# Second 16-head attention in a new order, its exponential at the eviction of the transposed scores, and the linear attention's end interleaved with the first cross attention

## The chip, the core and the metric

The kernel runs on one core of a Trainium2 chip. A core has five engines with a queue of instructions each: TensorE (PE: matrix products and transpositions, which go into eight PSUM banks), VectorE (DVE), ScalarE (ACT), GpSimd (POOL) and SyncE (SP), whose queue only starts transfers here. Every queue is written out by hand, and semaphores are all that orders one engine against another. The metric is device microseconds of one execution, lower being better.

## The reference

Two layers of a post-norm decoder over 16 sequences of 128 tokens and 256 features, in float32. Each of the six sublayers is added to its input and normalized:

```python
x = ln(x + linear_attention(x))      # A: 16 heads, rms norm of q and k, rotation, relu, no softmax
x = ln(x + cross_attention(x, ctx))  # B: one head, causal softmax
x = ln(x + sparse_ffn(x))            # C: 15 of 128 tokens of a sequence, 16-head attention and FFN
x = ln(x + self_attention(x))        # D: 16 heads of 16 features, softmax
x = ln(x + cross_attention(x, ctx))  # E: 16 heads of 16 features, causal softmax
x = ln(x + moe(x))                   # F: 16 experts, 4 of them per token, and two shared ones
```

D and E compute, for each sequence and each head, `softmax(q k^T * 16**-0.5) v`, and E also masks the keys behind the query. The first "16-head attention" of this text is D and the second is E. F's router is a product of the normalized result of E with a 256x16 matrix.

## The kernel before

A sequence (128 rows) is the unit of work and is called a turn, numbered 0 to 15. A stage is a function of a turn, with a lag: `pipelined` and `chained` run over iterations i and call each stage of their list for turn i minus its lag, in the list's order. Every engine has a list of its own, and what an iteration's list says is the order of that engine's queue. D and E are one `chained` loop of 32 turns on each engine, so that iterations 16 and above hold E's turn i - 16 for lag 0. Two places of the code matter most.

**The end of A and the begin of B.** A runs on PE as the list a_nd (lag 4), a_kv (3), a_qkp (0), a_atp (4), a_vp (1), a_op (4) in iterations 0 to 19. Behind it come four small products (`b_fold`) that multiply B's weight matrices with each other, two into bank 1 and two into bank 2, and then B's loop, which begins by transposing the normalized rows of turn 0 (b_turn). On ACT, A's last stage is a_final (lag 8, L1679), which writes the normalized row into X and needs the reciprocal root that POOL has worked out (a_power, L892 to L897, and DVE's y, L2041, waits for the a_final of two turns before, since there are two buffers). Behind all sixteen a_final stand the two copies of the folded weights (L1686, L1688) and then B's loop, with the copy of the transposed row (L1641) first. DVE's queue ends A with y, sum and statistics of turn 15, copies a column (L2096) and goes on to B's row maximum (L2059). The small first transfer of constants (cos and sin) and the second (identity, masks and others) are waited for as l_rows and l_const; DVE waits for both before its first work on a turn (L1994), POOL for l_const at its begin.

**A turn of D or E.** For four groups r of four heads each, PE computes the negated scores into banks 3 to 6 (L1493, and in E the mask, L1504). DVE takes the row minimum of each (L2416, L2418). For groups 0 to 2 ACT evicts the bank with `exp(min - s)`, four instructions of one head each (L1871); for group 3 DVE subtracts into SBUF (L2421) and ACT takes the exponential there (L1875). PE transposes the four heads of a group into bank 7 (d_pT, L1520), ACT copies the bank to SBUF (d_pTc, L1882), and since all groups share bank 7, group r + 1 is transposed only when group r is copied. Then PE multiplies with v (d_pv, L1530), DVE divides (d_div, L2427 to L2436), PE applies the output matrix (d_out), and DVE adds and takes statistics (d_y, L2443). The row transposition of a later turn (d_turn, L1036) and its projections (d_proj) stand in the same list; both write bank 1. In E the router of F follows three steps later in the same bank: f_turn transposes the normalized row (L1057), ACT copies it (f_copy, L1820), f_lg multiplies, and ACT copies the logits (f_logit, L1824). For turns 5 to 15 of E, d_turn waits until the logits of five turns before are copied, which are those of the same iteration (f_logit raises f_lc):

```python
def d_turn_(t, n=n, round=round):
    wait(pe, d_qkc.again(n), t, 4, back=1)
    if n == 1:
        wait(pe, f_lc, t, 1, back=5)
    turn_x(round, o=bank[1])(t)
```

From E's turn 9 on, DVE also does the first half of the routing between d_div and the next minimum (f_first_half).

## Time and profile before

| what | us |
|---|---|
| median of 3 runs | 896.17 |
| lowest and highest of them | 892.79, 896.87 |
| the profiled execution | 893.42 |
| its span, first to last instruction | 891.6 |

In that span PE is busy for 812.5 us (91%), DVE for 543.2, ACT for 509.6 and POOL for 457.4. The span falls into the linear attention A (to about 110), B (to about 185), C (to about 285), D (to about 405), E with the router (to about 560), the scattering of rows to the experts' lists (to about 645) and the experts with the final sum (to the end). Times below are microseconds from the begin of the span. A row of the timeline gives start, duration, engine, line, operation, output and inputs by the names of the program, shape and count; the bracket at its end is how long the engine stood idle before it and what released it. Most buffers are views of one tensor called arena.

### The profile page before, as it was taken

Reading aid. Unit: us, or ns where it says so; the run is one execution under the profiler, and the core shown is the slowest. Engines: PE = TensorE matmul, PEld = TensorE weight load, DVE = VectorE, ACT = ScalarE, POOL = GpSimd, SP = SyncE. Lnnn points to the kernel's source line nnn. Section 1 sums busy time; section 2 is a strip of 40 time slices with the busy share of each in tenths; the row PEclk is TensorE's granted clock in tenths of the full one; section 3 lists DMA queues with packets and bytes.
Section 4 is the critical chain, followed back from the end, with each engine's and each line's share of the span. In section 5 each row is a group of like instructions: output and inputs, shape, how many; then the busy total and the mean of one; then the engine's idle time right before and its main releaser. Section 6 shows DMA issues by size and latency. Waiting matters only on the chain.

```text
span 891.6 us, 21329 instructions
## 1 busy us (share of the span) xinstructions
PE 812.5 (91%) x6466; PEld 663.1 (74%) x6467; DVE 543.2 (61%) x1608; ACT 509.6 (57%) x1348; POOL 457.4 (51%) x609
## 2 busy tenths in 40 slices
PE   5989679998898999998999987999889999999995
PEld 2666569875687788877677765555889999999963
DVE  3788727857413788888877899586233333333325
ACT  2556445544524888888888866310555565556524
POOL 4988511201306465544456542777766555555545
PEclk9999989999799999999999999999999999999998
DMA  9620011000007999994611001637576555655556
GB/s 308 203 69 12 13 42 43 25 25 13 13 21 244 316 279 336 298 295 139 249 38 35 8 33 37 243 136 251 168 109 104 94 93 96 97 92 93 97 75 250
DMA packets 86645, 113.52 MB, mean 127 GB/s; under 512 B 8224, under 2 KB 77600, under 8 KB 86048
## 3 DMA queue, kind: packets, MB, share of 16 engines
q1 hardware_dynamic: 71392, 90.49, 33.7%
q0 software_dynamic: 14448, 19.34, 13.4%
q10 hardware_dynamic: 720, 2.63, 0.8%
q8 instruction: 44, 0.72, 0.4%
q14 instruction: 41, 0.34, 0.1%
HBM read 48.40 MB, written 64.05 MB: 126 GB/s over the span
## 4 chain that ended last, share of the span: by engine, by line
PE 57%; DVE 12%; POOL 11%; ACT 8%; issue 8%; DMA 4%; SPq 0%; DVEq 0%; ACTq 0%; POOLq 0%
PE bank L1044 39%; POOL grid L948 7%; PE bank L1520 4%; ACT arena L1871 4%; PE bank L1057 3%; PE bank L1493 3%; PE bank L1530 1%; DMA const<-in_const 1%; PE bank L1388 1%; ACT arena L1882 1%; POOL arena L894 1%; DMA arena<-ys 1%; DMA ys<-arena 1%; DVE arena L2416 1%; DVE arena L2006 1%
## 5 line engine op out<-in xcount | busy, mean ns | idle before, releaser
L1044 PE MATMUL bank<-arena 128*128 128x256 f32 (+6 forms) x1028 | 276.6, 403 | 13.8 <-ACT arena L1669 8.7
L1044 PEld LDWEIGHTS bank<-arena 128*128 128x128 f32 (+1 forms) x1028 | 175.5, 190 | 71.4 <-issue 38.1
L1004 POOL DMA_INDIRECT ys<-arena x79 | 123.1, 1558 | 95.1 <-DVE arena L2535 74.5
L1044 PEld LDWEIGHTS bank<-arena,rows 128*128 128x128 f32 x1264 | 153.5, 192 | 8.6 <-ACT arena L1910 3.2
L1044 PE MATMUL bank<-arena,rows 128*128 128x128 f32 x1264 | 155.8, 276 | 2.5 <-ACT arena L1910 2.5
L1871 ACT ACTIVATE arena<-bank,arena 128x128 f32<-128x128 f32 x384 | 114.0, 420 | 5.7 <-DVE arena L2416 5.6
L1920 ACT COPY rows<-arena 128x1024 f32 x79 | 82.6, 1045 | 33.3 <-issue 24.4
L2524 DVE TENSOR_TENSOR arena<-arena,bank 128x256 f32<-128x256 f32 x79 | 33.3, 422 | 106.1 <-ACT arena L1905 105.6
L853 POOL TENSOR_TENSOR lr<-mv,const 128x1 f32<-128x1 f32 x48 | 9.1, 191 | 171.8 <-DVE mv L1957 171.8
L1882 ACT COPY arena<-bank 128x512 f32<-128x512 f32 x128 | 79.8, 624 | 21.1 <-PE bank L1520 20.2
L1520 PE MATMUL bank<-const,arena 128*128 128x128 f32 x512 | 80.5, 280 | 12.4 <-ACT arena L1882 9.6
L1520 PEld LDWEIGHTS bank<-const,arena 128*128 128x128 f32 x512 | 56.1, 141 | 30.7 <-issue 20.4
L948 POOL DMA_INDIRECT grid<-X,arena x64 | 63.4, 991 | 20.2 <-issue 18.8
L1905 ACT ACTIVATE arena<-bank 128x256 f32<-128x256 f32 x79 | 30.4, 385 | 72.0 <-PE bank L1044 72.0
L2416 DVE TENSOR_REDUCE arena<-bank 128x4 f32<-128x512 f32 x96 | 62.2, 683 | 14.8 <-PE bank L1493 7.9
L1044 PE MATMUL bank<-arena,inT 128*128 128x256 f32 (+1 forms) x192 | 59.8, 436 | 9.3 <-DMA arena<-in_a_w 5.8
L1044 PE MATMUL bank<-xT,arena 128*128 128x128 f32 x512 | 66.5, 279 | 1.6 <-ACT xT L1641 1.6
L1044 PEld LDWEIGHTS bank<-xT,arena 128*128 128x128 f32 x512 | 62.3, 195 | 2.3 <-ACT xT L1641 2.3
L2535 DVE TENSOR_SCALAR arena<-bank,arena 128x256 f32<-128x256 f32 x79 | 38.2, 484 | 27.9 <-PE bank L1044 22.9
L1044 PEld LDWEIGHTS bank<-arena,inT 128*128 128x128 f32 x192 | 34.3, 198 | 18.9 <-issue 11.4
L1057 PE MATMUL bank<-const,arena 128*128 128x128 f32 x222 | 43.1, 276 | 4.4 <-DMA arena<-grid 2.3
L1836 ACT ACTIVATE arena<-bank 128x512 f32<-128x512 f32 x16 | 9.6, 598 | 63.8 <-PE bank L1044 63.8
(291 smaller groups left out, 1455.2 us busy)
## 6 DMA issues: line engine op xcount, KB each, us to landing
grid<-arena SPq DMA_DIRECT2D x1, 37264.0 KB, 133.9
arena<-in_f_w SPq DMA_DIRECT2D x18, 768.0 KB, 6.8
arena<-grid SPq DMA_DIRECT2D x79, 137.0 KB, 2.6
arena<-ys SPq DMA_DIRECT2D x8, 512.0 KB, 7.8
inT<-in_ctxT SPq DMA_DIRECT2D x30, 128.0 KB, 2.0
X<-in_x SPq DMA_DIRECT2D x1, 2048.0 KB, 15.7
arena<-in_c_w SPq DMA_DIRECT2D x2, 1024.0 KB, 5.4
ys<-arena SPq DMA_DIRECT2D x1, 2048.0 KB, 10.3
```

The costliest lines, as they stand in the source:

```text
L948: pool.indirect_dma_start(grid, bass.IndirectOffsetOnAxis(ap=f_to[:, b, k:k + 1], axis=0), X[:, b, :], None).then_inc(l_sc[b % 3], 16)
L1004: pool.indirect_dma_start(ys, bass.IndirectOffsetOnAxis(ap=number, axis=0), s_y[t.ring(YR)], None, compute_op=ALU.add).then_inc(l_sy[t.rin ...
L1044: m = pe.matmul(o, lhs[k], rhs[k], start=k == 0, stop=k == n - 1)
L1057: m = pe.transpose(o[:, k * width:(k + 1) * width], src(k), ident[0:width, 0:width])
L1520: m = pe.transpose(bank[7][:, i * P:(i + 1) * P], d_S[t.p][:, QH * r + i, :], ident)
L1871: m = act.activation(d_S[t.p][:, at, :], bank[3 + r][:, i * P:(i + 1) * P], ACT.Exp, bias=d_mx[t.p][:, at:at + 1], scale=-1.0)
L1882: act.copy(d_pT[t.p][:, QH * r:QH * (r + 1), :], bank[7][:].rearrange("p (a b) -> p a b", a=QH)).then_inc(d_pTc.sem, 1)
L1905: act.activation(f_h[t.p], bank[2 + t.p][:, 0:EF], ACT.Silu).then_inc(q_silu.sem, 1)
L1920: act.copy(f_up[t.p], W[:, bass.ds(e, 1), 0:2 * KC * EF].rearrange("p a n -> p (a n)")).then_inc(q_wc.sem, 1)
L2416: dve.tensor_reduce(mx, s_, AX.X, ALU.min).then_inc(dm.sem, 2)
L2524: dve.tensor_tensor(f_aT[t.p], f_h[t.p].rearrange("p (k t) -> p k t", k=KC), bank[2 + t.p][:, EF:2 * EF].rearrange("p (k t) -> p k t", k=K ...
L2535: dve.tensor_scalar(s_y[t.ring(YR)], bank[6 + t.p][:, 0:D], s_w[t.p], None, ALU.mult).then_inc(q_yc.sem, 1)
```

## The change

Four edits.

1. **Begin.** POOL's and DVE's waits for the second transfer of constants stand where the first of them is read: POOL's at the first a_power, DVE's at the first a_kvm.
2. **End of A.** The four folding products are taken into A's list on PE, one at the end of each of the iterations 16 to 19. ACT leaves A's loop with three a_final undone, copies the folded weights, enters B's loop and does the three at the ends of B's iterations 1, 2 and 3. DVE's first write of B's normalized row waits until all of A's are read.
3. **Exponential.** In D and E, ACT evicts the score banks 3 to 5 with `min - s` (Identity), DVE subtracts group 3 in that sense too, PE transposes these differences, and ACT takes the exponential when it evicts bank 7 (d_pTc). The separate exponential of group 3 (L1875) is gone, and the transposition of group 3 waits for DVE alone. The four evictions of group 2 are split: two as before at the end of an iteration, two in the next iteration behind the first d_pTc, where L1875 stood.
4. **Order of E.** On PE, d_out stands between the transpositions of groups 2 and 3, and f_lg behind that of group 3. On ACT, f_logit stands behind the eviction of group 1. D keeps its order.

The core of the diff:

```diff
-            chained(pe, [[(a_nd_, 4), (a_kv_, 3), (a_qkp_, 0), (a_atp_, 4), (a_vp_, 1), (a_op_, 4)]])
...
+            def b_fold_(i):
+                part = i - B
...
+                o, wl, wr = ((bank[1], b_wq, b_wk), (bank[2], b_wv, b_wp))[part // KC]
+                k = part % KC
+                m = product(o[:, k * D:(k + 1) * D], [wl[:, e, k * P:(k + 1) * P] for e in range(KC)],
+                            [wr[:, e, :] for e in range(KC)])
...
+            chained(pe, [[(a_nd_, 4), (a_kv_, 3), (a_qkp_, 0), (a_atp_, 4), (a_vp_, 1), (a_op_, 4)]], b_fold_)
...
-                        wait(pe, d_exp.again(n), t, r + 1)
+                        if direct(r):
+                            wait(pe, d_exp.again(n), t, r + 1)
+                        else:
+                            wait(pe, d_max.again(n), t, 2 * r + 2)
...
-                               (last(f_lg_), 7), (d_pT_(3), 5), (d_out_, 6), (d_turn_, 2), (d_pv_, 5), (last(f_first_pos_), 5),
+                               (last(d_out_), 6), (d_pT_(3), 5), (d_out_ if n == 0 else None, 6), (last(f_lg_), 7),
+                               (d_turn_, 2), (d_pv_, 5), (last(f_first_pos_), 5),
...
-            pipelined(act, [(a_final_, 8), (a_osq_, 5), (a_fTc_, 3), (a_sq_, 1), (a_relu_, 2), (a_atc_, 4)])
+            pipelined(act, [(a_final_, 8), (a_osq_, 5), (a_fTc_, 3), (a_sq_, 1), (a_relu_, 2), (a_atc_, 4)], left=A_LEFT)
...
+            def a_rest_(i):
+                if 0 < i <= A_LEFT:
+                    a_final_(turn(B - 1 - A_LEFT + i))
...
-                        act.copy(d_pT[t.p][:, QH * r:QH * (r + 1), :],
-                                 bank[7][:].rearrange("p (a b) -> p a b", a=QH)).then_inc(d_pTc.sem, 1)
+                        act.activation(d_pT[t.p][:, QH * r:QH * (r + 1), :], bank[7][:].rearrange("p (a b) -> p a b", a=QH),
+                                       ACT.Exp).then_inc(d_pTc.sem, 1)
...
-                rounds.append([(last(h_fill_(0)), 6), (d_pTc_(0), 5), (d_exp_(3), 5), (d_qkc_, 3),
+                early, late = range(QH // 2), range(QH // 2, QH)
+                rounds.append([(last(h_fill_(0)), 6), (d_pTc_(0), 5), (d_exp_(2, heads=late), 5), (d_qkc_, 3),
...
-                               (last(f_logit_), 7), (d_pTc_(3), 5), (d_exp_(1), 4),
-                               (copy_xT(round, before, reader, bank[1]), 2), (d_exp_(2), 4),
+                               (d_pTc_(3), 5), (d_exp_(1), 4), (last(f_logit_), 7),
+                               (copy_xT(round, before, reader, bank[1]), 2), (d_exp_(2, heads=early), 4),
```

ACT's queue in a turn of E, before. L1882 is d_pTc, L1871 the eviction of the scores of a group (one head and then three), L1820 f_copy, L1824 f_logit, L1641 the copy of the row that d_turn has transposed:

```order
L1820 COPY arena<-bank 128x256 [waits f_tp]
L1882 COPY arena<-bank 128x512 [waits d_pv,d_pTp]
L1871 ACTIVATE arena<-bank,arena 128x128 [waits d_pTp,d_max]
L1871 ACTIVATE arena<-bank,arena 128x128 x3
L1824 COPY arena<-bank 128x16 [waits f_lp]
L1882 COPY arena<-bank 128x512 [waits d_pv,d_pTp]
L1871 ACTIVATE arena<-bank,arena 128x128 [waits d_pTp,d_max]
L1871 ACTIVATE arena<-bank,arena 128x128 x3
L1641 COPY xT<-bank 128x256 [waits d_qkp,turned]
```

The same stretch of ACT's queue now, where the lines are L1837 (f_copy), L1896 (d_pTc), L1886 (evictions), L1841 (f_logit) and L1652:

```order
L1837 COPY arena<-bank 128x256 [waits f_tp]
L1896 ACTIVATE arena<-bank 128x512 [waits d_pv,d_pTp]
L1886 ACTIVATE arena<-bank,arena 128x128 [waits d_pTp,d_max]
L1886 ACTIVATE arena<-bank,arena 128x128 x3
L1896 ACTIVATE arena<-bank 128x512 [waits d_pv,d_pTp]
L1886 ACTIVATE arena<-bank,arena 128x128 [waits d_pTp,d_max]
L1886 ACTIVATE arena<-bank,arena 128x128 x3
L1841 COPY arena<-bank 128x16 [waits f_lp]
L1652 COPY xT<-bank 128x256 [waits d_qkp,turned]
```

The copy of the logits has moved from the place behind the first four evictions to the place behind the next d_pTc and four more evictions.

PE's queue in the same turn now, from the transposition of group 2 on (L1530 is d_pT, L1044 with 128x256 d_out, with 128x16 f_lg, L1036 d_turn, L1540 d_pv):

```order
L1530 MATMUL bank<-const,arena 128x128 [waits d_pTc,d_exp]
L1530 MATMUL bank<-const,arena 128x128 x3
L1044 MATMUL bank<-arena 128x256 [waits d_y,d_atc]
L1044 MATMUL bank<-arena 128x256
L1530 MATMUL bank<-const,arena 128x128 [waits d_pTc,d_max]
L1530 MATMUL bank<-const,arena 128x128 x3
L1044 MATMUL bank<-arena 128x16 [waits f_xt]
L1044 MATMUL bank<-arena 128x16
L1036 MATMUL bank<-const,xs 128x128 [waits copied,xt_done,f_lc,d_qkc]
L1036 MATMUL bank<-const,xs 128x128
L1540 MATMUL bank<-arena 32x128 [waits d_pTc,e_vc,d_bk]
```

Before, f_lg stood behind the first of these transpositions and d_out behind the second; d_turn with its wait for f_lc, and d_pv behind it, stand last in both.

PE's queue at the end of A now (L1092 is a_nd, L1057 from arena a_atp, L1044 waiting for a_ob a_op, the other L1044 folding products, L1057 from X the first of B):

```order
L1044 MATMUL bank<-arena 128x256 [waits a_ob,a_atc]
L1044 MATMUL bank<-arena 128x256
L1044 MATMUL bank<-arena 128x256 [waits a_vb]
L1044 MATMUL bank<-arena 128x256
L1092 MATMUL bank<-arena 128x136 [waits a_div,a_fTc,a_kvm]
L1092 MATMUL bank<-arena 128x136
L1057 MATMUL bank<-const,arena 128x128 [waits a_atc,a_div]
L1057 MATMUL bank<-const,arena 128x128
L1044 MATMUL bank<-arena 128x256 [waits a_ob,a_atc]
L1044 MATMUL bank<-arena 128x256 x3
L1057 MATMUL bank<-const,X 128x128 [waits normed]
```

Before, no folding product stood ahead of a_nd, and all of them stood behind the last a_op.

ACT's queue at the same place before (L1674 is a_osq, L1693 and L1699 are B's copy of the queries and its exponential):

```order
L1674 ACTIVATE arena<-arena 128x256 [waits a_pow,a_ob]
L1679 ACTIVATE X<-y,arena 128x256 [waits a_pow] x3
L1686 ACTIVATE arena<-bank 128x512 [waits b_fold]
L1688 COPY arena<-bank 128x512 [waits b_fold]
L1641 COPY xT<-bank 128x256 [waits turned] x2
L1693 COPY arena<-bank 128x256 [waits b_qp]
L1641 COPY xT<-bank 128x256 [waits b_qp,turned]
L1699 ACTIVATE arena<-arena 128x128 [waits b_max]
```

And now, with a_osq on L1687, a_final on L1692, the copies of the weights on L1699 and L1701, of the rows on L1652, of the queries on L1706:

```order
L1687 ACTIVATE arena<-arena 128x256 [waits a_pow,a_ob]
L1699 ACTIVATE arena<-bank 128x512 [waits b_fold]
L1701 COPY arena<-bank 128x512 [waits b_fold]
L1652 COPY xT<-bank 128x256 [waits turned] x2
L1706 COPY arena<-bank 128x256 [waits b_qp]
L1692 ACTIVATE X<-y,arena 128x256 [waits a_pow]
L1652 COPY xT<-bank 128x256 [waits b_qp,turned]
L1712 ACTIVATE arena<-arena 128x128 [waits b_max]
```

The three a_final have moved from the place ahead of the copies of the folded weights into B's loop, of which the first is seen here.

## Rows read from the trace of the kernel before

**Rows 1.** Timeline of the first 14 us: start, duration, engine, line, operation, count [idle].

```profile
12.23 0.69 DVE L1994 TENSOR_TENSOR arena<-bank,rows 128x512 f32<-128x512 f32 x1 [2.12 <-DMA const<-in_const]
```

**Rows 2.** Timeline from the end of A to the first turns of B.

```profile
103.24 0.63 PE L1092 MATMUL bank<-arena 128*128 128x136 f32 x4
...
103.91 0.17 DVE L2021 TENSOR_SCALAR arena<-bank 128x16 f32<-128x16 f32 x1
...
105.78 4.58 PE L1044 MATMUL bank<-arena 128*128 128x256 f32 x20 [0.46 <-ACT arena L1669]
...
107.41 0.42 ACT L1674 ACTIVATE arena<-arena 128x256 f32<-128x256 f32 x1 [0.20 <-DVE arena L2036]
...
109.96 0.60 ACT L1679 ACTIVATE X<-y,arena 128x256 f32<-128x256 f32 x1 [2.04 <-POOL arena L897]
...
110.66 0.48 DVE L2041 SCALAR_TENSOR_TENSOR y<-arena,rows 128x256 f32<-128x256 f32 x1 [1.60 <-ACT X L1679]
...
112.30 0.26 DVE L2096 COPY arena<-cols 128x256 f32<-128x256 f32 x1
...
115.78 0.58 ACT L1686 ACTIVATE arena<-bank 128x512 f32<-128x512 f32 x1
...
117.25 0.66 PE L1057 MATMUL bank<-const,X 128*128 128x128 f32 x2 [6.67 <-ACT xT L1641]
...
117.70 1.91 PE L1044 MATMUL bank<-xT,arena 128*128 128x128 f32 x8
...
121.51 0.29 DVE L2059 CUSTOM_DVE_ANT_0 arena<-bank,const 128x128 f32<-128x128 f32 x1 [8.96 <-PE bank L1044]
...
123.66 0.27 PE L1151 MATMUL bank<-const,arena 128*128 128x128 f32 x1
```

**Rows 3.** Stretches, busy us (count) of PE, PEld, DVE, ACT, POOL; granted clock, DMA.

```profile
117.20:121.90 4.70, 4.14 (x18) 3.91 (x19) 0.30 (x2) 0.87 (x3) 0.00 (x0) 0.50 0.00 0
297.00:331.00 34.00, 33.99 (x371) 28.07 (x371) 28.38 (x66) 28.61 (x90) 16.84 (x33) 1.00 1.12 289
503.00:560.00 57.00, 47.02 (x550) 33.53 (x550) 52.82 (x138) 37.37 (x109) 23.87 (x41) 1.00 0.09 29
```

**Rows 4.** Timeline of one turn of E with the router in it.

```profile
468.72 1.06 PE L1044 MATMUL bank<-xT,arena 128*128 128x128 f32 x8
...
470.00 0.63 PE L1520 MATMUL bank<-const,arena 128*128 128x128 f32 x4 [0.22 <-ACT arena L1882]
...
472.23 0.60 PE L1520 MATMUL bank<-const,arena 128*128 128x128 f32 x4
...
473.35 1.15 ACT L1871 ACTIVATE arena<-bank,arena 128x128 f32<-128x128 f32 x4
...
474.36 0.20 ACT L1824 COPY arena<-bank 128x16 f32<-128x16 f32 x1
474.42 0.64 ACT L1882 COPY arena<-bank 128x512 f32<-128x512 f32 x1
...
474.93 0.38 PE L1036 MATMUL bank<-const,xs 128*128 128x128 f32 x2
...
475.91 0.45 ACT L1641 COPY xT<-bank 128x256 f32<-128x256 f32 x1
...
476.25 0.66 PE L1520 MATMUL bank<-const,arena 128*128 128x128 f32 x4
```

**Rows 5.** Chain that ended last: the scores of two turns of E, seven turns apart.

```profile
438.51 1.07 PE bank L1493 x16
...
494.71 1.07 PE bank L1493 x16
```

**Rows 6.** Timeline where DVE's routing begins, in E's late turns.

```profile
499.22 0.42 DVE L2443 TENSOR_TENSOR y<-bank,arena 128x256 f32<-128x256 f32 x1 [1.03 <-PE bank L1044]
...
508.30 1.08 PE L1530 MATMUL bank<-arena 128*32 128x128 f32 x32
...
510.01 0.71 DVE L2427 STREAM_TRANSPOSE arena<-bank 128x512 f32<-128x512 f32 x1
```

More of the change, by code:

```diff
@@ L210, in wait_end, with pipelined @@
     eng.wait_ge(step.sem, step.end())
-def pipelined(eng, stages, start=0, stop=B, peel=0):
+def pipelined(eng, stages, start=0, stop=B, peel=0, left=0):
     deepest = max(lag for _, lag in stages)
@@ L231, in pipelined @@
                 stage(Turn(2 * j + b, b % 2, j + b // 2))
-    for i in range(stop, stop + deepest):
+    for i in range(stop, stop + deepest - left):
         iteration(i)
@@ L268, in rolled, with chained @@
         iteration(i)
-def chained(eng, rounds):
+def chained(eng, rounds, also=None):
     deepest = max(lag for _, lag in rounds[0])
@@ L280, in chained @@
                 rounds[b // B][k][0](turn(b % B))
+        if also is not None:
+            also(i)
 def build(nc, a):
@@ L1642, in copy_xT @@
                 return stage
+            A_LEFT = 3
             def a_sq_(t):
@@ L2010, in a_kvm_ @@
                 wait(dve, a_nd, t, 1, back=2)
+                if t.peeled and t.b == 0:
+                    dve.wait_ge(l_const, 16)
                 kv = bank[3][:, 0:KC * VW].rearrange("p (k n) -> p k n", k=KC)
```

46 lines of the change are left out of this document (23 added, 23 removed).

## Prediction

> **What bounds the kernel now.** I first read the busy shares by stage, then the chain that ended last, then the timeline where the diff acts, because PE's 91% is a mean of stages with different limits. Four places count. At the begin, DVE sits 2.12 us before its first work on a turn, released by the second transfer of constants [rows 1]. Between A and B, PE stands idle for 6.67 us until ACT has copied a transposed row, and then works at a granted clock of 0.50, the lower level of 1.2 GHz [rows 2, 3]. In D, PE is busy for 33.99 of 34.00 us while ACT has 28.61 and DVE 28.38 [rows 3]: PE's own work is the limit there. In E with the router, the scores of two turns lie 56.20 us apart over seven turns, 8.03 each [rows 5], and the turn is a ring of PE and ACT: PE's second transposition waits 0.22 us for ACT's first copy, the first eviction follows the third transposition by 1.12 us (472.23 to 473.35), and so on [rows 4]. In E's last turns the limit is DVE, 52.82 of 57.00 us [rows 3].
>
> **Begin.** With the wait moved, DVE starts when its own preparation is done. The 2.12 us are idle time that only the transfer ends, and POOL's first work waits for DVE's first result. POOL then reads the constants behind two products, some 3 us later, when they are there. I take -2.1; bounds: -2.1, and -1.4 if POOL or the next transposed input is late by a third of it.
>
> **End of A.** The folding products are 16 of the 20 in the row at 105.78, which takes 4.58: 0.92 for four, so 0.9 for each part [rows 2]. They are not put into PE's free time: each stands behind the output product of an iteration and ahead of the next a_nd, and DVE's division starts 0.04 after a_nd ends (103.24 + 0.63, 103.91) [rows 2]. So three of the four parts lengthen the tail by 0.9 each, 2.7, and turn 15's output product starts at 108.5 instead of 105.78; the fourth ends at about 110.4, where the folding ended before (105.78 + 4.58). Then:
> ACT squares turn 15 at 107.41 + 2.7 = 110.1, to 110.7, and goes straight to the copies of the weights. From these to PE's work for B it was 117.25 - 115.78 = 1.47 [rows 2], now 112.2. Three a_final were in between; they are hidden in B only if ACT has time there. The first of them is ready at 109.96 + 2.7 = 112.7, but ACT takes it only after B's first copy of queries, about 113.9 (PE's eight products for it take 1.06 at the higher level [rows 4], ACT's copy 0.4). It ends at about 114.5. Waiting behind it is DVE's y of turn 15, which started 0.10 after it (109.96 + 0.60, 110.66): 114.6, 3.9 later than before. Behind y come A's last statistics, the column copy (112.30 + 3.9 = 116.2, with 0.26) and B's first row maximum, 116.5 instead of 121.51. Maximum (0.29), exponential and hand-overs take about 1.0, an estimate, so PE's first transposition of B's probabilities starts at 117.5 instead of 123.66 [rows 2]: -6.2. Before, PE arrived at 123.66 fully occupied; now it also waits for ACT's next copy, 0.2. I take -6.0. From there B runs in its old order. The other two a_final cost ACT 0.6 each in B, where PE is the limit. Bounds: -7.5 (PE loses the whole 6.67 us of idleness and the eight products at 1.91 instead of 1.06) and -2 (rival 3).
>
> **Exponential and the split in D.** Each turn loses ACT's 128x512 exponential; the eviction of bank 7 keeps its shape and gets another function (0.64 as a copy [rows 4]). PE issues the same instructions. As D is PE's [rows 3], this is worth 0; bounds -1 and +1 over the 16 turns, since ACT has 5 us in 34 to spare.
>
> **E.** Two effects of opposite sign. **Gain:** with two evictions instead of four ahead of it, the first d_pTc no longer holds back PE's second transposition. That wait is 0.22 now, and PE cannot come sooner than the projection's end; I take 0.25 a turn (bounds 0.2 and 0.3). Four turns have it without the router: -1.0.
> **Loss:** d_turn waits for f_logit of the same iteration, and f_logit has moved behind d_pTc and four evictions. The block it has been moved past is 475.91 - 474.42 = 1.49 us of ACT, which is busy without a gap from 473.35 on [rows 4]. Its start moves from 474.36 to 475.85, less the 0.25 gained earlier: 475.6. It takes 0.20 and about 0.05 to hand over, so d_turn starts at 475.85 instead of 474.93 [rows 4]. Queued behind d_turn on PE are d_pv and everything that follows: the next turn's first transposition comes 1.32 after d_turn (476.25). So a turn gets 0.9 longer net of the gain, 8.9 instead of 8.03. The d_out that has moved ahead gives nothing: it only lets PE reach the wait sooner. d_turn waits so for turns 5 to 15 of E, 11 iterations. In the first 8 PE and ACT are the limit: +7.2 (bounds 0.6 and 1.1 a turn, +4.8 and +8.8). In the last 3, DVE is: its transposition starts 0.63 after d_pv ends (508.30 + 1.08, 510.01), so 1.49 later means 0.86 a turn, +2.6; but the 1.03 that DVE waited for d_out where this stretch begins falls away, since d_out comes earlier [rows 6]. I take +1.5 (bounds 0 and +2.6). E together: -1.0 + 7.2 + 1.5 = +7.7.
> The Trainium skill's page "PSUM — Partial Sum Buffer", section "Engine vs sequencer instructions", says that ScalarE's queue is strictly first in, first out and that matmuls start in program order, even though weight loads may run ahead. By that rule nothing on PE passes the waiting d_turn, and the sum stands; if products could pass it, E would be -3 instead of +7.7 (rival 1).
>
> **Sum.** -2.1 - 6.0 + 0 + 7.7 = -0.4 us. The rows are of the execution of 893.42, whose span is 891.6; the sum on it is 893.0. The median shown, 896.17, lies 2.75 above; the four executions known (892.79, 893.42, 896.17, 896.87) have a mean of 894.8, and I put the sum on that: **894.4**. No work behind E has a clock of its own: the scatters start with DVE's places.
>
> **Rivals.**
> 1. *E's order costs nothing.* If the logits are in time for d_turn, the 0.25 of the shorter wait holds in all turns: -2.1 - 6.0 - 1.0 - 8 x 0.25 = -11, 883.7. For it: today d_turn starts 0.4 us after f_logit has ended and isn't held by it [rows 4]. Against it: the wait's count, and 1.49 us of ACT between.
> 2. *Slower: PE's clock falls in E.* PE now stands 1.5 to 2 us before d_turn in each of 11 turns, and a turn's PE work is some 7 us. If the granted clock fell to 0.50 for a third of it in eight turns, as after the 6.67 us of idleness between A and B, that is 8 x 2.3 = +19, 913. It decides from 0.6 us a turn, where the sum passes +4.5. Against it: in 503 to 560 PE works for 47.02 of 57.00 us, with 10 us of gaps in six turns, and the clock stays at 1.00 [rows 3].
> The Trainium skill's page "TensorE: Matmul & The Clock Gate", section "What's actually happening", says that the array's default is the throttled clock and that activity releases it. By that rule waits in PE speak against this change; what the rows show for gaps of this size is the full clock, and only the 6.67 us shows the lower one.
> 3. *The hand-over pays a third.* ACT takes the undone a_final between B's first copies, DVE waits with y, and if PE's lower clock of 117.20 to 121.90 comes back there, two more us are lost: -2 instead of -6, so +3.6, 898.4. For it: PE stays half idle between 110.4 and 117.5. Against it: no gap there is longer than some 2 us.
>
> **How the numbers follow.** Forecast 0.68, rival 1 0.13, rival 2 0.05, rival 3 0.14. A difference of 0.5%, 4.5 us, is about what a measurement of this kernel can tell from no change. The forecast's own bounds are -4.5 (small loss in E, full gain at the hand-over) and +4 (large loss in E), on executions that differ by 4 us among themselves. The range takes these and rival 3: 888.5 to 899.5. Faster by over 0.5%: rival 1 and the forecast's lower edge, 0.18. Slower: rival 2 and parts of rival 3 and of the upper edge, 0.10. Within: 0.72.
>
> **What would show it.** In the profile after: DVE's first work on a turn at about 10.1; PE's first transposition of B's probabilities some 8 us earlier than 123.66; D's turns unchanged; E's turns at 8.9 with PE waiting before d_turn for the copy of the logits. Turns of E at 7.8 or less would refute the main loss; turns of B at clock 0.50 or a first row maximum after 118 would refute the hand-over.

## The result, and the profile after

The changed kernel takes 902.79 us (median of ten executions, 900.79 to 909.88) against 896.34 of the kernel before (ten, 892.79 to 900.70). The ratio of the two means is 1.0094, with an interval of 1.0060 to 1.0128: slower by 0.9%, where the prediction had 894.4, no difference, and a range that ended at 899.5. The profiled execution took 909.57, with a span of 907.8. A second profiled execution (run after_again, below) took 903.92, with a span of 902.1.

Where the time went is read from PE's rows in the timelines: the first transposition of B's probabilities (L1151 before, L1158 after) and the scores of D's and E's turns (L1493, L1500). Differences from the kernel before are in brackets.

| stretch | before | after | after, again | forecast |
|---|---|---|---|---|
| start to B's first transposition of probabilities | 123.66 | 115.16 (-8.50) | 115.49 (-8.17) | -8.1 |
| to D's first scores (rest of B, and C) | 159.36 | 162.18 (+2.82) | 160.05 (+0.69) | 0 |
| to the scores of D's turn 14 | 116.93 | 117.29 (+0.36) | 117.31 (+0.38) | 0 |
| five turns, to E's turn 3 | 38.49 | 37.27 (-1.22) | 37.28 (-1.21) | -1.0 |
| eight turns, to E's turn 11 | 64.56 | 82.31 (+17.75) | 80.85 (+16.29) | +7.2 |
| four turns, to E's turn 15 | 37.18 | 38.94 (+1.76) | 39.06 (+1.88) | +1.5 |
| to the end of the span | 351.42 | 354.65 (+3.23) | 352.06 (+0.64) | 0 |
| span | 891.6 | 907.8 (+16.2) | 902.1 (+10.5) | -0.4 |

So begin, hand-over, D and the four turns without the router came as forecast. The miss is one row: the eight turns of E with the router. Their windows in the profile after (columns as in [rows 3]: stretch, its length, busy time and count of PE, PEld, DVE, ACT, POOL, granted clock, DMA) have two kinds of turn:

```profile
417.05:424.54 7.49, 6.71 (x96) 5.24 (x95) 6.34 (x14) 5.92 (x19) 3.49 (x8) 1.00 0.27 89
442.39:452.86 10.47, 8.89 (x101) 7.14 (x101) 6.22 (x12) 6.57 (x21) 4.46 (x8) 0.84 0.00 1
463.30:472.27 8.97, 7.39 (x101) 5.87 (x101) 5.85 (x12) 6.48 (x21) 4.18 (x8) 1.00 0.16 66
472.27:482.75 10.48, 8.90 (x101) 7.32 (x100) 6.50 (x13) 6.50 (x21) 5.58 (x10) 0.84 0.01 2
```

The first row is a turn without the router: 7.49, where before it was 7.74. The third is a turn with the router at the full clock: 8.97, the 8.9 that the prediction worked out against 8.03 [rows 5]. The second and the fourth are the others: the same work, 1.5 us longer, at a mean granted clock of 0.84. Nine of the eleven turns in which d_turn waits for the logits are of this kind, in both profiled executions. The timeline of one such turn shows where the clock falls (start, duration, engine, line; the bracket is the idle time before):

```profile
435.42 0.52 PE L1044 MATMUL bank<-arena 128*128 128x16 f32 x4
435.70 0.62 ACT L1896 ACTIVATE arena<-bank 128x512 f32<-128x512 f32 x1
436.18 1.18 ACT L1886 ACTIVATE arena<-bank,arena 128x128 f32<-128x128 f32 x4
...
437.17 0.24 ACT L1841 COPY arena<-bank 128x16 f32<-128x16 f32 x1
437.52 0.41 PE L1036 MATMUL bank<-const,xs 128*128 128x128 f32 x2 [1.58 <-issue]
437.86 1.74 PE L1540 MATMUL bank<-arena 128*32 128x128 f32 x32
...
439.52 1.12 PE L1530 MATMUL bank<-const,arena 128*128 128x128 f32 x4
...
440.44 1.59 PE L1044 MATMUL bank<-xT,arena 128*128 128x128 f32 x8
```

PE finishes the logits product at 435.94. ACT copies the logits only at 437.17, behind d_pTc (L1896) and four evictions (L1886), and d_turn (L1036) starts 1.58 after PE's last work. The products behind it then take 1.74, 1.12 and 1.59 where the kernel before has 1.08, 0.66 and 1.06 for them [rows 4, 6]. The clock falls while the first of them runs, to the lower of its two levels, 1.2 GHz instead of 2.4, and is back at the full one before the next scores; between the two it stands at 0.50:

```profile
439.52:440.44 0.92, 0.92 (x9) 0.92 (x5) 0.76 (x2) 0.00 (x0) 0.77 (x3) 0.50 0.00 0
```

The waits view of PE over nine of E's router turns (431 to 525) names one place, and the chain that ended last runs through it in each of the eleven ("issue" because the profile names no releaser for it):

```profile
PE bank L1036 <- issue: 14.2, 9, 1.6
```

```profile
435.93 1.58 issue
437.93 1.67 PE bank L1540 x32
...
446.42 1.58 issue
```

At the hand-over, the profile after answers [rows 2] so:

```profile
106.65 1.99 PE L1044 MATMUL bank<-arena 128*128 128x256 f32 x8 [0.46 <-ACT arena L1682]
...
110.16 0.41 PE L1057 MATMUL bank<-const,X 128*128 128x128 f32 x2 [1.30 <-ACT xT L1652]
110.41 1.06 PE L1044 MATMUL bank<-xT,arena 128*128 128x128 f32 x8
...
111.77 0.60 ACT L1692 ACTIVATE X<-y,arena 128x256 f32<-128x256 f32 x1
...
112.47 0.48 DVE L2059 SCALAR_TENSOR_TENSOR y<-arena,rows 128x256 f32<-128x256 f32 x1 [2.54 <-ACT X L1692]
...
114.29 0.28 DVE L2077 CUSTOM_DVE_ANT_0 arena<-bank,const 128x128 f32<-128x128 f32 x1
...
115.16 0.33 PE L1158 MATMUL bank<-const,arena 128*128 128x128 f32 x1 [0.53 <-ACT arena L1712]
```

PE stands idle for 1.30 instead of 6.67, the eight products take 1.06 instead of 1.91, and B's first row maximum (L2077) is at 114.29 instead of 121.51.

### The profile page after: what moved, and what is told of

It reads as the page before. It is cut to its first block, busy times and chain, and to the rows that moved or that the text cites. A ratio compares the mean times of both kernels' runs of the same rounds, so it can differ in the third digit from the quotient of the medians.

```text
span 907.8 us, 21329 instructions
## 1 busy us (share of the span) xinstructions
PE 824.4 (91%) x6466; PEld 675.4 (74%) x6467; DVE 541.8 (60%) x1608; ACT 497.8 (55%) x1316; POOL 457.6 (50%) x609
## 4 chain that ended last, share of the span: by engine, by line
PE 66%; POOL 10%; DVE 8%; issue 8%; ACT 4%; DMA 3%; SPq 0%; DVEq 0%; ACTq 0%; POOLq 0%
PE bank L1044 43%; POOL grid L948 7%; PE bank L1530 7%; PE bank L1540 4%; PE bank L1057 3%; PE bank L1500 3%; DMA const<-in_const 1%; PE bank L1395 1%; DMA arena<-ys 1%; PE bank L1036 1%; DMA ys<-arena 1%; DVE arena L2022 1%; PE bank L1237 1%; PE bank L1166 1%; ACT arena L1896 1%
## 5 line engine op out<-in xcount | busy, mean ns | idle before, releaser
L1044 PE MATMUL bank<-arena 128*128 (+6 forms) x1028 | 278.4, 406 | 13.2 <-ACT arena L1682 8.5
L1044 PEld LDWEIGHTS bank<-arena 128*128 128x128 f32 (+1 forms) x1028 | 177.0, 191 | 69.2 <-issue 39.6
L1044 PEld LDWEIGHTS bank<-arena,rows 128*128 128x128 f32 x1264 | 155.3, 195 | 8.6 <-ACT arena L1925 3.0
L1044 PE MATMUL bank<-arena,rows 128*128 128x128 f32 x1264 | 157.4, 279 | 2.5 <-ACT arena L1925 2.5
L1886 ACT ACTIVATE arena<-bank,arena 128x128 f32<-128x128 f32 x384 | 115.5, 395 | 3.1 <-DVE arena L2434 3.0
L1896 ACT ACTIVATE arena<-bank 128x512 f32<-128x512 f32 x128 | 77.5, 605 | 41.6 <-PE bank L1530 40.5
L1530 PE MATMUL bank<-const,arena 128*128 128x128 f32 x512 | 84.7, 291 | 5.8 <-ACT arena L1896 5.8
L1530 PEld LDWEIGHTS bank<-const,arena 128*128 128x128 f32 x512 | 59.6, 147 | 26.9 <-issue 12.7
L1044 PE MATMUL bank<-xT,arena 128*128 128x128 f32 x512 | 69.3, 286 | 1.8 <-ACT xT L1652 1.8
L1044 PEld LDWEIGHTS bank<-xT,arena 128*128 128x128 f32 x512 | 65.6, 204 | 2.5 <-ACT xT L1652 2.5
L1044 PE MATMUL bank<-arena,inT 128*128 128x256 f32 (+1 forms) x192 | 60.0, 437 | 7.6 <-DMA arena<-in_a_w 6.0
L1044 PEld LDWEIGHTS bank<-arena,inT 128*128 128x128 f32 x192 | 34.4, 199 | 17.3 <-issue 9.7
L1057 PE MATMUL bank<-const,arena 128*128 128x128 f32 x222 | 43.0, 276 | 4.4 <-DMA arena<-grid 2.4
L972 POOL TENSOR_TENSOR arena<-arena,const 128x256 f32<-128x256 f32 x64 | 40.8, 658 | 9.2 <-ACT arena L1874 9.2
```

What stands on the lines that cost most here:

```text
L972: pool.tensor_tensor(d_kx[t.p][:, k], kT[:, k:k + 1, :].to_broadcast([P, 2, P]), c("pairs").unsqueeze(2).to_broadcast([P, 2, P]), ALU.mult ...
L1044: m = pe.matmul(o, lhs[k], rhs[k], start=k == 0, stop=k == n - 1)
L1057: m = pe.transpose(o[:, k * width:(k + 1) * width], src(k), ident[0:width, 0:width])
L1530: m = pe.transpose(bank[7][:, i * P:(i + 1) * P], d_S[t.p][:, QH * r + i, :], ident)
L1886: m = act.activation(d_S[t.p][:, at, :], bank[3 + r][:, i * P:(i + 1) * P], ACT.Identity, bias=d_mx[t.p][:, at:at + 1], scale=-1.0)
L1896: act.activation(d_pT[t.p][:, QH * r:QH * (r + 1), :], bank[7][:].rearrange("p (a b) -> p a b", a=QH), ACT.Exp).then_inc(d_pTc.sem, 1)
```

## The experiments

The theory after the result (W, and C for its second half): E loses because d_turn waits on PE for the copy of the logits, once by the wait's length and once more by the clock behind it. The first rival (X): not the order but the new exponential makes E slow.

All ratios are against the kernel before, run on the same chip. The expectations speak of ten and of four turns at the lower clock where the windows, turn by turn, give nine of the changed kernel and five of wait_filled, and of 14 turns with the wait of wait_added where the timeline has 16; these miscounts were mine.

### Is it E's order or the exponential?

**old_order_e** puts back E's order and leaves all the rest changed:

```diff
-                               (last(d_out_), 6), (d_pT_(3), 5), (d_out_ if n == 0 else None, 6), (last(f_lg_), 7),
+                               (last(f_lg_), 7), (d_pT_(3), 5), (d_out_, 6),
...
-                               (d_pTc_(3), 5), (d_exp_(1), 4), (last(f_logit_), 7),
+                               (last(f_logit_), 7), (d_pTc_(3), 5), (d_exp_(1), 4),
```

> The changed kernel with E's order of before on TensorE and ScalarE (logits product and copy of the logits where they stood); begin, end of A and the exponential stay changed. In the changed kernel a turn of E with the router takes 10.46 us, of which TensorE waits 1.58 before d_turn, and behind that wait it works at a granted clock of 0.50 in most turns (turn 463 to 472, where it stays 1.00: 8.97). Theory W, the wait: without it the turns with the router go to 7.7 to 7.9 at a clock of 1.00; over the twelve turns 431.90 to 553.15 that is 22 to 26 us less than the 121.25 of the changed kernel, and the time is 882 to 888. Theory X, the exponential: if it is the move of the exponential or the split of group 2 that makes E slow, the turns stay above 9.5 and the time at 898 to 905.

883.2, ratio 0.9862 (0.9839 to 0.9885). A turn with the router in it:

```profile
444.37:452.07 7.70, 7.54 (x101) 5.96 (x100) 6.12 (x13) 6.36 (x21) 4.70 (x9) 1.00 0.01 2
```

7.70 at the full clock, PE busy for 7.54 of it. Theory X falls: the exponential's move does no harm to E, the order does it all. This is also the fastest kernel of this study, 1.4% below the kernel before.

**order_only** makes the same edit on the kernel before, alone:

```diff
-                               (last(f_lg_), 7), (d_pT_(3), 5), (d_out_, 6), (d_turn_, 2), (d_pv_, 5), (last(f_first_pos_), 5),
+                               (last(d_out_), 6), (d_pT_(3), 5), (d_out_ if n == 0 else None, 6), (last(f_lg_), 7),
+                               (d_turn_, 2), (d_pv_, 5), (last(f_first_pos_), 5),
...
-                               (last(f_logit_), 7), (d_pTc_(3), 5), (d_exp_(1), 4),
+                               (d_pTc_(3), 5), (d_exp_(1), 4), (last(f_logit_), 7),
```

> The kernel before with E's new order alone: d_out between the transpositions of groups 2 and 3, the logits product behind group 3, the copy of the logits behind the eviction of group 1. The exponential of group 3 stays where it was. Theory W: TensorE waits 1.2 to 1.7 us before d_turn in each turn with the router as in the changed kernel, and works at 0.50 behind it in most of them: turns of 10.3 to 10.8 instead of 8.03, +19 to +25, 914 to 920. If the wait costs its own length alone: turns of 9.0 to 9.4, 903 to 908. Theory X, the order does no harm without the exponential's move: 893 to 898.

912.5, ratio 1.0197 (1.0169 to 1.0226). The rows of one turn:

```profile
446.39:456.89 10.50, 8.91 (x102) 7.25 (x101) 6.52 (x13) 7.08 (x22) 5.44 (x10) 0.84 0.01 2
```

```profile
449.90 0.52 PE L1044 MATMUL bank<-arena 128*128 128x16 f32 x4
...
452.01 0.41 PE L1036 MATMUL bank<-const,xs 128*128 128x128 f32 x2 [1.59 <-issue]
452.35 1.84 PE L1530 MATMUL bank<-arena 128*32 128x128 f32 x32
```

The same wait, 1.59, and the same lower clock behind it, in eight of eleven turns. Some 18 us are the order's. The time lies below the 914 to 920 that was expected, with three turns at the full clock.

### Where the logits' copy would have to stand

**logit_middle** moves the copy of the logits one place forward on ACT:

```diff
-                               (d_pTc_(3), 5), (d_exp_(1), 4), (last(f_logit_), 7),
+                               (d_pTc_(3), 5), (last(f_logit_), 7), (d_exp_(1), 4),
```

> The changed kernel with the copy of the logits one place earlier on ScalarE: behind the last d_pTc, ahead of the eviction of group 1. By the changed kernel's rows (logits product ends at 435.94, d_pTc of group 3 at 436.18, d_turn at 437.52) TensorE would wait some 0.6 before d_turn instead of 1.58. Theory W with a wait that costs its own length alone: turns of 8.0 at clock 1.00, 887 to 892. If a wait of 0.6 is enough for the clock of 0.50 behind it: turns of 9.0 to 9.5, 897 to 902. Theory X: 898 to 905 with a wait that has shrunk.

884.55, ratio 0.9881 (0.9859 to 0.9903), below the expected 887 to 892. PE's wait is 0.56, and in nine turns with the router the clock stays at 1.00 and the turn is as long as expected:

```profile
448.63 0.41 PE L1036 MATMUL bank<-const,xs 128*128 128x128 f32 x2 [0.56 <-issue]
```

```profile
444.04:451.98 7.94, 7.38 (x102) 5.85 (x101) 5.93 (x13) 6.38 (x21) 4.74 (x9) 1.00 0.01 2
```

So one place on ACT is worth 18 us of the changed kernel's 902.8. A turn is shorter by 1.03 than the 8.97, which is the wait's own length (1.58 - 0.56 = 1.02); the other 1.5 a turn are the clock's. In the last two turns with the router DVE is the limit and PE waits longer: behind 2.45 the clock stays at 1.00, behind 2.39 in the next turn the mean is 0.74.

**logit_early** puts both back to where the copy is in time for certain, and keeps the early d_out:

```diff
-                               (last(d_out_), 6), (d_pT_(3), 5), (d_out_ if n == 0 else None, 6), (last(f_lg_), 7),
+                               (last(f_lg_), 7), (last(d_out_), 6), (d_pT_(3), 5), (d_out_ if n == 0 else None, 6),
...
-                               (d_pTc_(3), 5), (d_exp_(1), 4), (last(f_logit_), 7),
+                               (last(f_logit_), 7), (d_pTc_(3), 5), (d_exp_(1), 4),
```

> The changed kernel with the logits product ahead of d_out and of the transposition of group 3 on TensorE, and the copy of the logits back behind the eviction of group 0 on ScalarE; d_out keeps its new place between the transpositions of groups 2 and 3. TensorE then has 1.7 us of its own work (1.03 and 0.63) between the logits product and d_turn, more than ScalarE needs to copy them. Theory W: no wait before d_turn, clock 1.00, turns with the router 7.5 to 7.8, time 881 to 887; the early d_out saves up to 0.2 a turn against the old order. Theory X: time at 898 to 905.

887.55, ratio 0.9909 (0.9882 to 0.9936): theory W holds, but my turn of 7.5 to 7.8 was 8.10. A new wait took the old one's place:

```profile
449.60 0.38 PE L1036 MATMUL bank<-const,xs 128*128 128x128 f32 x2
...
450.54 1.08 PE L1540 MATMUL bank<-arena 128*32 128x128 f32 x32 [0.56 <-ACT arena L1896]
```

With 1.58 of other products ahead of it, the transposition of group 3 comes so late that d_pv (L1540) waits for ACT's copy of it. The early d_out saves nothing by itself: the old order is 0.40 a turn shorter. One late turn of this run, where DVE is the limit and PE waits before d_turn, has the lower clock, though no logits product stands next to the wait; what stands there is the transposition of group 3:

```profile
508.41 0.41 PE L1036 MATMUL bank<-const,xs 128*128 128x128 f32 x2 [1.78 <-issue]
```

```profile
502.31:513.48 11.17, 9.22 (x102) 7.44 (x101) 10.48 (x28) 6.66 (x21) 5.94 (x11) 0.85 0.22 73
```

### What lowers the clock?

The wait's own length explains 8.97. Three runs ask why the clock falls behind it. **wait_filled** lets PE make the logits product three times instead of once:

```diff
-                product(bank[1][:, D:D + E], [f_xT[:, t.b, k, :] for k in range(KC)],
-                        [f_rw[:, k, :] for k in range(KC)]).then_inc(f_lp.sem, 1)
+                for again in range(3):
+                    m = product(bank[1][:, D:D + E], [f_xT[:, t.b, k, :] for k in range(KC)],
+                                [f_rw[:, k, :] for k in range(KC)])
+                m.then_inc(f_lp.sem, 1)
```

> The changed kernel, only that TensorE does the logits product three times, twice for nothing, into the same place: 1.04 us of useless products lie where it waited before d_turn, and 0.5 us of wait is left, since ScalarE copies the logits only behind the eviction of group 1. Theory C, the clock falls because TensorE stands still: the wait's length between useful work stays, but the clock stays at 1.00, so turns take 8.9 to 9.0 instead of 10.46 and the time is 889 to 895, less than the changed kernel with more work. Rival: if the clock falls for another reason (the share of useful work over a turn is the same), the turns stay at 10.4 or above and the time at 900 to 910.

**wait_wide** fills the same place with four products of 128x240:

```diff
-                        [f_rw[:, k, :] for k in range(KC)]).then_inc(f_lp.sem, 1)
+                        [f_rw[:, k, :] for k in range(KC)])
+                product(bank[1][:, D + E:2 * D], [f_xT[:, t.b, k, :] for k in range(KC)],
+                        [d_w[1][:, k, 3 * D + E:4 * D] for k in range(KC)]).then_inc(f_lp.sem, 1)
```

> The changed kernel with four useless products of 128x240 (some 1.0 us, by the 1.03 of the 128x256 form) between the logits product and d_turn, where the run with eight more logits products of 128x16 still showed the clock at 0.50 in four of eleven turns. ScalarE's order is untouched, so d_turn starts no earlier; the wait left is some 0.55 us. Theory C, the clock falls when TensorE does little in that place: with wide products the clock stays at 1.00 in every turn, 8.9 to 9.0 us each instead of 10.46, and the time is 890 to 896. Rival, the wait itself or the useful work per turn decides: four or more turns at 10.4 and 897 to 904.

wait_filled took 898.39, ratio 1.0033 (1.0012 to 1.0054); wait_wide 893.09, ratio 0.9976 (0.9962 to 0.9991). The first lies between the two times that were expected, the second in theory C's. Both do more work than the changed kernel and both are faster than it, by 4 and by 10 us. A turn of wait_filled, and one of wait_wide (the group of eight there is the logits product's four and the four wide ones, under the shape of the first):

```profile
489.68 1.41 PE L1044 MATMUL bank<-arena 128*128 128x16 f32 x12
491.78 0.41 PE L1036 MATMUL bank<-const,xs 128*128 128x128 f32 x2 [0.69 <-issue]
492.12 1.70 PE L1542 MATMUL bank<-arena 128*32 128x128 f32 x32
```

```profile
441.13 1.42 PE L1044 MATMUL bank<-arena 128*128 128x16 f32 x8
443.23 0.41 PE L1036 MATMUL bank<-const,xs 128*128 128x128 f32 x2 [0.68 <-issue]
443.57 1.08 PE L1542 MATMUL bank<-arena 128*32 128x128 f32 x32
```

And the windows, first a turn of wait_filled at the lower clock, then of wait_wide five turns in one row, and its one turn at the lower clock:

```profile
486.16:496.64 10.48, 9.79 (x109) 8.13 (x108) 6.49 (x13) 6.55 (x21) 5.57 (x10) 0.84 0.18 72
```

```profile
446.58:491.46 44.88, 41.45 (x521) 32.31 (x521) 30.92 (x61) 32.39 (x101) 23.51 (x41) 1.00 0.11 37
519.30:530.87 11.57, 9.84 (x105) 7.57 (x104) 9.06 (x22) 6.59 (x21) 5.31 (x9) 0.85 0.01 1
```

The two fillings take the same time (1.41 and 1.42) and leave the same wait (0.69 and 0.68), so PE's busy share is the same (8.28 and 8.29 of 8.97 in a turn at the full clock). Behind the narrow products the clock fell in five of eleven turns; behind the wide ones it stayed at 1.00 in ten of eleven, and fell in the one late turn (519.30) in which DVE, the limit there, made PE wait 1.73. In the nine turns before DVE is the limit, where the waits are the 0.69 and 0.68, it is three against none. This is no matter of single executions: the mean granted clock of the whole lies at 0.976 to 0.980 in ten executions of wait_filled and at 0.983 to 0.990 in ten of wait_wide. The rival of theory C, that useful work per turn decides, falls: it is the same in both.

**wait_added** makes a wait without the router's products next to it, in the fastest kernel:

```diff
                     if n == 1:
                         wait(pe, f_lc, t, 1, back=5)
+                        wait(pe, d_exp.again(n), t, 2, back=2)
```

> The kernel with E's order of before and the other edits kept (883.2), and one wait more: d_turn of E also waits until ScalarE has evicted group 1 of the same iteration, which nothing there needs. TensorE's order and work stay. By that kernel's rows d_turn starts at 448.75 and the eviction ends at 449.90, so it waits some 1.2 to 1.4 us in 14 turns, with and without the router. Theory C, the wait itself lowers the clock: turns of 10.0 to 10.6 instead of 7.45 and 7.70, the clock 0.50 behind the wait, 14 turns of +2.5: 912 to 920. Rival, the clock falls only with what else the changed kernel has: turns of 8.7 to 9.1, 898 to 903.

902.84, ratio 1.0094 (1.0067 to 1.0121). One window from D's last scores to E's last, d_turn in a turn with the router, and the turn with the longest wait:

```profile
401.12:546.53 145.41, 119.00 (x1551) 89.98 (x1551) 108.02 (x226) 102.12 (x312) 68.39 (x121) 1.00 0.17 61
```

```profile
448.20 1.03 PE L1044 MATMUL bank<-arena 128*128 128x256 f32 x4
...
450.43 0.41 PE L1036 MATMUL bank<-const,xs 128*128 128x128 f32 x2 [1.20 <-issue]
```

```profile
525.05 0.41 PE L1036 MATMUL bank<-const,xs 128*128 128x128 f32 x2 [2.72 <-issue]
```

My theory C in the form "the wait itself lowers the clock" fell here. In the eleven turns with the router PE waits 1.20 in eight and 1.53, 2.72 and 2.13 in the others, directly behind d_out's products of 128x256, and the clock stays at 1.00 in all of them. A turn grows from 7.70 to 9.10, a little more than the wait; the kernel is as slow as the changed one, since the wait stands in 16 turns and not in eleven. The other profiles say the same: old_order_e has waits of 1.74 and 1.66 in this place, and with the pairs of the five other kernels in E's old order 28 waits of 1.0 to 2.7 us stand directly behind d_out, all at 1.00. So the length of the wait does not decide. Together with the pair above: in E the clock fell only where something else stood between d_out and the wait. E's new order put the transposition of group 3 and the logits product there, since it took d_out away from the place ahead of d_turn.

Three things stay open. No run separates the narrow logits product from that transposition: logit_early's late turn has the lower clock with the transposition alone between d_out and the wait. Wide products in between are no sure remedy: wait_wide's 1.73 lowered the clock, its 1.60 a turn before did not. And the same wait of 1.58 leaves the clock alone in two turns of eleven, as 1.96 does in one late turn of the changed kernel; no run here shows why.

### The other edits

**begin_end** has the first two edits alone, **exp_only** the third alone, **begin_only** the first, and **begin_left** the first and, of the second, only the three a_final left for B. The diffs are those parts of the change; the one that matters is begin_left's, which keeps ACT's part of the second edit and leaves the folding products behind A:

```diff
-            pipelined(act, [(a_final_, 8), (a_osq_, 5), (a_fTc_, 3), (a_sq_, 1), (a_relu_, 2), (a_atc_, 4)])
+            pipelined(act, [(a_final_, 8), (a_osq_, 5), (a_fTc_, 3), (a_sq_, 1), (a_relu_, 2), (a_atc_, 4)], left=A_LEFT)
```

> The kernel before with the first two edits alone (the wait for the second constants; folding products in A's list and three a_final left for B). In the changed kernel the first transposition of B's probabilities starts at 115.16 instead of 123.66, and D's first scores at 277.34 instead of 283.02; between them, in C, TensorE works at a granted clock of 0.66 for 7.70 us where the kernel before has 1.00. Theory H, the hand-over pays all it shows and the loss in C is a matter of single executions: 8.5 off the profiled 893.42, and 886 to 889. Rival: the work that starts earlier is given back in C each time, 5.7 is left: 889 to 892.

887.34, ratio 0.9919 (0.9890 to 0.9948), some 7 us: within the interval the hand-over pays what it shows, 8.94. B's first transposition of probabilities is at 114.72 and D's first scores at 273.45, 158.73 apart. The rival, that C gives the gain back, falls: over the profiled runs of the study this distance lies between 158.7 and 162.2, and not by kernel (159.36 before, 161.90 in begin_only, 162.18 and 160.05 in the two executions of the changed kernel, 158.98 in wait_wide).

> The kernel before with the first edit and of the second only the three a_final that are left for B; the four folding products stay in one block behind A. By rows of the kernel before, moved 1.6 earlier, the block ends at 108.8, the copies of the weights at 109.9, and the first a_final in B's loop ends at about 113; the first transposition of B's probabilities then starts at 115.9 to 116.5 against 115.16 with the folding products interleaved too. Theory L, leaving the a_final is what pays: time within 2 of the run with both edits (887.3). Rival F, the folding products' new place pays: 890 to 894.

885.49, ratio 0.9904 (0.9874 to 0.9933). PE's last products of A with the folding in them, and its first transposition of B's probabilities:

```profile
104.90 4.58 PE L1044 MATMUL bank<-arena 128*128 128x256 f32 x20 [0.46 <-ACT arena L1671]
...
115.52 0.33 PE L1151 MATMUL bank<-const,arena 128*128 128x128 f32 x1 [0.53 <-ACT arena L1701]
```

115.52 against 115.16: with the folding in one block of 4.58 the hand-over is as early. Theory L holds. The whole gain comes from the a_final that ACT leaves for B; the new place of the folding products moves B's start by 0.8 us at most (114.72 in begin_end), and the time by nothing that can be measured (0.9904 against 0.9919).

> The kernel before with the first edit alone. In the changed kernel VectorE's first work on a turn starts at 10.60 instead of 12.23. Theory: A is paced by the chain that starts there, so the 1.6 last to the end: first transposition of B's probabilities near 122.0, the time 1 to 2 below the kernel before. Rival: a later transfer or POOL sets A's pace and the 1.6 are given back before B: no difference.

895.38, ratio 0.9994 (0.9976 to 1.0013). DVE's first turn started at 10.26 instead of 12.23 and B's first transposition of probabilities at 121.21 instead of 123.66, but the time of the whole shows no difference; the interval still holds the 1.6.

> The kernel before with the third edit alone (exponential at the eviction of bank 7, group 2's evictions split; E's order of before). By the kernel with E's order of before and all else changed (883.2, turns of E with the router 7.70) against 8.03 of the kernel before: 0.33 for each of eight turns and 0.25 to 0.3 for four without the router, -3.5 to -4, D unchanged at 8.45: 891 to 893. Rival, the edits pay only together: 894 to 897. If the first two edits are worth less than 8.5, this one must be worth more, down to 887.

894.26, ratio 0.9988 (0.9966 to 1.0010). In the profile E's turns with the router go from 8.03 to 7.70 and D's first fourteen take 117.31 instead of 116.93; from D's first scores to E's last that is 254.13 against 257.16, 3.0 less, of which the ratio shows 1. Unclear by itself: nothing lies within the interval, and the expected 3.5 to 4 just outside its end of 3.0. A second pair is on record. old_order_e has the first three edits and begin_end the first two, and their ratios, 0.9862 (0.9839 to 0.9885) and 0.9919 (0.9890 to 0.9948), do not meet; from D's first scores to E's last they take 254.08 and 256.92. With the hand-over in place the third edit is worth some 3 us by the profiles and 5 by the ratios.

> The changed kernel once more, for another profiled execution: ten executions lay at 900.8 to 904.6 (seven) and 909.6 to 909.9 (three), and the one read had ten of eleven turns with the router at the clock of 0.50. Theory W: a lower time has fewer of these turns, 1.5 us for each, so an execution of 902 has five or six of them; nothing else moves by more than 2 us. Rival: the difference of 7 lies in C or in the experts and E's turns are as in the first profile.

903.92 in one execution. It has nine turns at the lower clock, as many as the first, so theory W's explanation of the spread among executions falls, and the rival is nearer: of the 5.7 us between the two spans, 1.46 are in the eight turns of E, 2.13 in C and 2.59 behind E. In the first execution C had a stretch at a mean clock of 0.66 that the kernel before has at 1.00 (first the profile after, then the kernel before, at the same work):

```profile
200.70:208.40 7.70, 7.70 (x18) 3.80 (x17) 4.69 (x23) 2.34 (x5) 0.00 (x0) 0.66 0.01 2
```

```profile
209.10:214.40 5.30, 5.30 (x19) 3.08 (x18) 4.65 (x24) 2.35 (x5) 0.00 (x0) 1.00 0.01 3
```

## Why the prediction was wrong, point by point

**What held.** *Begin:* -2.1 was forecast; DVE's first turn starts 1.63 earlier in one execution and 2.20 in the other; alone, in begin_only, it is 2.45 at B's first transposition of probabilities and nothing that can be measured in the whole. *Hand-over:* with the begin taken off, the steps put turn 15's last product at 106.4, the first a_final in B at 111.8, y of turn 15 at 112.5, the row maximum at 114.4 and PE's transposition at 115.4 to 115.6; the rows have 106.65, 111.77, 112.47, 114.29 and 115.16. Rival 3 is out: the lower clock did not come back (1.06 for the eight products). The folding products lengthen A's tail as worked out, and begin_left shows what follows from that: they could have stayed. *D:* 0 within 1, measured +0.36. *E's gain:* -1.0, measured -1.2. *E's loss at the full clock:* a turn of 8.9, measured 8.97. d_turn was held by f_logit, with d_pv and all that follows behind it; in wait_wide, where the clock stays at 1.00, the eight turns take 71.80, +7.2 as forecast. *E's last turns:* +1.5, measured +1.8, but partly by luck: two of the four ran at the lower clock in one execution and three in the other, which the forecast did not have.

**What failed.** Rival 2, PE's clock, was given a chance of 0.05, and it came. Its mechanism and its place were named, and its price (8 x 2.3, which is 18.4 and not 19) was too high: the clock costs 1.5 in a turn that has it (10.47 - 8.97), 9 to 10.5 over the eight turns. The failing step is the reason against it: that between 503 and 560 PE has 10 us of gaps in six turns and the clock stays at 1.00 [rows 3]. That is a sum, and because of it the +7.2 for the eight turns was priced at the full clock alone. Taken apart, the kernel before has two waits there that come near the one forecast, before the same instruction; one of them, and what stands ahead of it:

```profile
515.19 1.03 PE L1044 MATMUL bank<-arena 128*128 128x256 f32 x4
517.67 0.41 PE L1036 MATMUL bank<-const,xs 128*128 128x128 f32 x2 [1.45 <-issue]
518.21 1.08 PE L1530 MATMUL bank<-arena 128*32 128x128 f32 x32
```

A wait of 1.45 at the full clock, but behind d_out's wide products. In the changed kernel d_out has moved, and the transposition of group 3 and the four products of 128x16 stand there. I compared lengths of gaps and not what PE does next to them; "the d_out that has moved ahead gives nothing: it only lets PE reach the wait sooner" was half of what that move does. wait_added and the pair wait_filled and wait_wide show the other half.

Nor was it so that only the 6.67 us showed the lower clock. In C of the same trace PE waits 2.03 behind products of 32x240, and then works at 0.50 for 10 us:

```profile
224.23 0.65 PE L1298 MATMUL bank<-const,arena 120*120 120x120 f32 x4 [2.03 <-ACT arena L1766]
```

```profile
225.00:235.00 10.00, 8.48 (x62) 6.98 (x63) 6.06 (x10) 7.01 (x14) 5.92 (x6) 0.50 0.00 0
```

The Trainium skill's page "TensorE: Matmul & The Clock Gate", section "What's actually happening", was cited with the prediction and set aside: throttled is the default, and activity releases it. The trace of the changed kernel agrees with that rule (0.50 behind the 1.58 us) where the argument from [rows 3] did not hold. The same page of the Trainium skill, section "A second HAM failure mode: psum-queue depth-cycling", tells of a kernel in which short idle times between groups of products, coming often enough, let the clock swing between its levels; this was not weighed, and the turns here do just that, lower behind nine of the eleven such waits and full again by the next scores (1.15 for them in turns of either kind).

**The sum.** By the parts measured alone, begin and end are -0.8%, the exponential -0.1% and the order +2.0%, together some +1.0%, against +0.9% for all of them: they add up. They are not independent: with begin and end in place the exponential is -0.6%, and on top of these three the order is +2.4% (1.0094 against 0.9862). On the profile the forecast's +7.2 for the eight turns should have been +16.3 to +17.8. The profiled execution of before also lay low: 351.42 behind E's last scores is the least of all profiled runs (352.1 to 355.1 in the others), and the sum had been put on 894.8, while the median of ten is 896.34.

## What to carry to other kernels

When an edit moves an instruction that another engine waits for, work out the wait in the new order, and then look at the work that stands next to it on the waiting engine: here a wait of 1.58 behind a transposition and narrow products brought the lower clock in nine turns of eleven and 1.5 us more in each, while waits of 1.0 to 2.7 directly behind d_out's wide products never did, and cost a turn little more than their length (1.40 for 1.20). To judge whether a clock will hold, look in the old trace, in all its stages, for single waits of that length with that neighbour, not for a sum of gaps. Of a bundle of edits run each alone, and the last also on top of the others: here one of the parts (what ACT leaves for the next stage) carried most of the gain, one ate it twice over, one (the exponential) showed its 3 to 5 us only beside the others, and two (the begin and the place of the folding products) were worth nothing that can be measured.

## What was not expected of the hardware

- Products that do nothing useful made the kernel faster: four of 128x240 ahead of a wait took 10 us off 902.8 (893.09), since the clock stayed at 1.00 in ten of eleven turns, behind waits of 0.68 to 1.60.
- At equal busy time and wait ahead of d_turn (0.69 and 0.68) the clock fell in three of nine turns behind products of 128x16 alone, and in none of nine behind products of 128x240; with the late turns, whose waits are longer, it is five and one of eleven.
- Directly behind d_out's products of 128x256 a wait of as much as 2.72 us left the clock at 1.00.
- The exponential as ACT's eviction of a 128x512 bank costs no more than a copy did: 605 ns on the mean of 128 against 624. The groups after and before:

```profile
L1896 ACT ACTIVATE arena<-bank 128x512 f32<-128x512 f32 x128 | 77.5, 605 | 41.6 <-PE bank L1530 40.5
```

```profile
L1882 ACT COPY arena<-bank 128x512 f32<-128x512 f32 x128 | 79.8, 624 | 21.1 <-PE bank L1520 20.2
```
